# Openings of the two head attentions moved into the stages before them, and the program's first loads reordered

## The reference

```python
x = x + jnp.tanh(g_xattn[0]) * _L0_xattn_ref(_layernorm(x, axis=-1), ctx_4096, ...)   # windowed attention
x = x + jnp.tanh(g_ffn[0]) * _L0_ffn_ref(_layernorm(x, axis=-1), ...)                 # mixture, top 2 of 8
x = x + jnp.tanh(g_xattn[1]) * _L1_xattn_ref(_layernorm(x, axis=-1), ctx_4096, ...)   # 32 heads, 4 of keys
x = x + jnp.tanh(g_ffn[1]) * _L1_ffn_ref(_layernorm(x, axis=-1), ...)                 # mixture, threshold
x = x + jnp.tanh(g_xattn[2]) * _L2_xattn_ref(_layernorm(x, axis=-1), ctx_4096, ...)   # one text head
x = x + jnp.tanh(g_ffn[2]) * _L2_ffn_ref(_layernorm(x, axis=-1), ...)                 # ternary weights
x = x + jnp.tanh(g_xattn[3]) * _L3_xattn_ref(_layernorm(x, axis=-1), ctx_4096, ...)   # 32 heads, 8 of keys, normed
x = x + jnp.tanh(g_ffn[3]) * _L3_ffn_ref(_layernorm(x, axis=-1), ...)                 # soft mixture
```

## Time and profile before

| what | us |
|---|---|
| median of 3 runs (3540.18 to 3541.86) | 3541.75 |
| the profiled execution | 3532.72 |
| its span, first to last instruction | 3530.9 |
| TensorE busy in it | 3308.4 (94%) |
| VectorE busy | 1845.0 (52%) |
| ScalarE busy | 1480.9 (42%) |
| GpSimd busy | 1088.2 (31%) |

### The profile page before, as it was taken

The page is one execution under the profiler, slowest core; times in us unless marked ns, Lnnn a source line. Parts: engine busy times, 40 slices in busy tenths (PEclk is TensorE's granted clock), DMA queues, the critical chain, the costliest instruction groups (busy, mean ns, idle before and its releaser), DMA issues. The chain is left out here.

```text
span 3530.9 us, 50041 instructions
## 1 busy us (share of the span) xinstructions
PE 3308.4 (94%) x19010; PEld 2778.4 (79%) x19010; DVE 1845.0 (52%) x3681; ACT 1480.9 (42%) x3318; POOL 1088.2 (31%) x632
## 2 busy tenths in 40 slices
PE   6999988999999999999988875999999999999996
PEld 5888864888888888888864654888788878888885
DVE  5788764333433343333344465555655565555554
ACT  4444422444444444444432443444344444444443
POOL 4333312223322322322321212333333333333323
PEclk9999999999999999999999897999999999999998
DMA  2000001122222212112100202122212212222201
GB/s 100 1 1 1 1 22 64 64 64 66 72 66 67 72 60 66 66 61 66 54 28 28 95 12 87 63 66 66 83 62 66 84 60 67 70 66 66 72 30 54
DMA packets 56657, 199.64 MB, mean 57 GB/s; under 512 B 9088, under 2 KB 9856, under 8 KB 53120
## 3 DMA queue, kind: packets, MB, share of 16 engines
q1 hardware_dynamic: 56448, 196.80, 16.7%
HBM read 192.58 MB, written 4.19 MB: 56 GB/s over the span
## 5 line engine op out<-in xcount | busy, mean ns | idle before, releaser
L1562 POOL TENSOR_TENSOR h_wol<-h_ro,h_woh 128x1024 fp32r<-128x1024 f32 x128 | 314.3, 2456 | 609.2 <-ACT h_woh L1612 609.2
L2046 DVE COPY h_tf<-ps 128x512 f32<-128x512 f32 (+1 forms) x256 | 142.5, 557 | 613.3 <-PE ps L1827 613.3
L1558 POOL TENSOR_TENSOR h_wql<-h_rq,h_wqh 128x1024 fp32r<-128x1024 f32 x128 | 308.9, 2414 | 483.4 <-ACT h_wqh L1607 483.4
L2050 DVE TENSOR_TENSOR h_ol<-ps,h_oh 128x512 fp32r<-128x512 f32 x256 | 177.0, 691 | 527.1 <-ACT h_oh L1665 526.9
L131 PE MATMUL ps<-h_woh,h_oh 128*128 128x512 f32 x1024 | 427.5, 418 | 5.7 <-DVE h_ol L2050 5.7
L131 PE MATMUL ps<-h_Xh,h_wqh 128*128 128x512 f32 x1024 | 414.2, 404 | 1.8 <-ACT h_sq L1651 0.8
L133 PE MATMUL ps<-h_woh,h_ol 128*128 128x512 f32 x1024 | 404.9, 395 | 0.0
L132 PE MATMUL ps<-h_wol,h_oh 128*128 128x512 f32 x1024 | 403.6, 394 | 0.0
L133 PE MATMUL ps<-h_Xh,h_wql 128*128 128x512 f32 x1024 | 401.3, 392 | 0.0
L132 PE MATMUL ps<-h_Xl,h_wqh 128*128 128x512 f32 x1024 | 401.1, 392 | 0.0
L1716 ACT ACTIVATE h_ex<-ps,h_mx 128x128 f32<-128x128 f32 x512 | 181.4, 366 | 269.6 <-DVE h_mx L2086 269.6
(11 more groups left out here) (287 smaller groups left out, 6754.6 us busy)
## 6 DMA issues: line engine op xcount, KB each, us to landing
h_rq<-in_L_Wq SPq DMA_DIRECT2D x128, 512.0 KB, 3.5
h_ro<-in_L_Wo SPq DMA_DIRECT2D x128, 512.0 KB, 3.5
h_rk<-in_L_Wkv SPq DMA_DIRECT2D x48, 512.0 KB, 3.5
h_craw<-in_ctxT SPq DMA_DIRECT2D x8, 1024.0 KB, 5.3
cnat<-in_ctx SPq DMA_DIRECT2D x4, 1024.0 KB, 11.0
t_craw<-in_ctxT SPq DMA_DIRECT2D x4, 1024.0 KB, 5.2
t_cn<-in_ctx SPq DMA_DIRECT2D x4, 1024.0 KB, 5.8
out_rows<-x SPq DMA_DIRECT2D x16, 256.0 KB, 2.2
```

Source lines behind the costliest of these rows:

```text
L1558: nc.gpsimd.tensor_tensor(wql[:, par], rq[:, par], f(wqh[:, par]), ALU.subtract).then_inc(m["p_wq"], 1)
L1562: nc.gpsimd.tensor_tensor(wol[:, par], ro[:, par], f(woh[:, par]), ALU.subtract).then_inc(m["p_wo"], 1)
L2046: nc.vector.tensor_copy(tf[:], ps[:, TBK, 0:PT]).then_inc(m["v_t"], 1)
L2050: nc.vector.tensor_tensor(by_head(ol), ps[:, AB, :].rearrange("p (b h t) -> p b h t", h=2, t=S), f(by_head(oh)), ALU.subtract).then_inc(m[ ...
```

## The change

- The program's first loads: the first context group now comes before the weights, and TensorE waits for 11 small constants and six quarter weights; the output weights, the next group of x and the 13 other loads follow, with semaphores of their own (`l_wo`, `l_late`). ScalarE loads one table set for logarithm and exponential at the start, and Tanh of the gates moves into the loop, behind the second exponential of the first tile.
- `phase_heads` becomes a generator: up to `yield opening` it makes the tiles of the opening (`h_ch`, `h_cl`, `h_wkh`, `h_wkl`, `h_xn` and small ones) and an object whose methods issue the opening's loads, splits, statistics, root and scaled rows. The stage in front (mixture 0 for heads 1, the text stage for heads 3) calls them in its own queues; the rest comes behind the barrier. The semaphores of both head attentions live to the program's end.
- In the heads stage, the first half of the first keys no longer waits for `v_xl`, and with `norm` the second block of keys and values goes to another bank, so that it follows the first at once.
- In the text stage, keys and queries are now single f32 products without splits. Context has two buffers, and the feed-forward weights have buffers of their own, which later take the opening's loads.

```diff
+                        sp.dma_start(cnat[:, 0:NT], a["ctx"][0]).then_inc(l_ct[0], 16)
+                        weights(("q", "k", "v"), l_w)
                         for dst, src in loads:
                             sp.dma_start(dst, src).then_inc(l_c, 16)
+                        weights(("o",), l_wo)
+                        sp.dma_start(x[:, NT:2 * NT], a["x"][1]).then_inc(l_x[1], 16)
+                        for dst, src in late:
+                            sp.dma_start(dst, src).then_inc(l_late, 16)
...
+                        nc.scalar.preload_act_table_set(LN_EXP)
                         act_root(act, 0)
...
+                                    else:
+                                        act.wait_ge(l_late, 16 * len(late))
+                                        nc.scalar.activation(tg[:], gates[:], ACT.Tanh).then_inc(c_a, 1)
+                                        nc.scalar.preload_act_table_set(LN_EXP)
...
                                 nc.gpsimd.tensor_tensor(x[:, i], x[:, i], tbias[:], ALU.add).then_inc(p_xb, 1)
+                                if opening and i == NT - 1:
+                                    opening.pool_keys(pool)
+                                if opening and i in (2 * NT - 1, 3 * NT - 1):
+                                    opening.pool_context(pool, (0, 1) if i < 2 * NT else (2, 3))
...
+                                if g == 0:
+                                    opening.act_keys(act)
+                                if g in (1, 2):
+                                    opening.act_context(act, (2 * g - 2, 2 * g - 1))
+                                if g == G - 1:
+                                    opening.rows_root(act)
...
+                            elif opening:
+                                opening.rows_stats(dve)
                             weigh(g)
+                            if opening and not more:
+                                opening.rows_out(dve)
                         add_output(G - 1)
...
-                                    last = passes(pe, ps[:, 4 + e % 2, :], wh[:, 1, c, cols(e)], wl[:, 1, c, cols(e)], ch[:, c], cl[:, c],
-                                                  c == 0, c == NC - 1)
+                                    last = nc.tensor.matmul(ps[:, 4 + e % 2, :], wr[:, 1, c, cols(e)], craw[:, g % 2, c],
+                                                            start=(c == 0), stop=(c == NC - 1))
...
+                            elif g + 2 == G:
+                                opening.rows_stats(dve)
+                            else:
+                                opening.rows_out(dve)
                             dve.wait_ge(s_t, g + 1)
                             nc.vector.tensor_copy(tf[:], ps[:, 3, :].rearrange("p (j k) -> p j k", j=NT)).then_inc(v_t, 1)
-                            if g + 1 < G:
-                                low(g + 1)
...
+                    def loads(self, sp):
+                        sp.dma_start(self.rk.rearrange("p c n -> p (c n)"), wkv[0]).then_inc(m["l_kv"], 16)
+                        sp.dma_start(self.craw, a["ctxT"][0]).then_inc(m["l_ct"], 16)
...
+                                if half and at(it, 0):
+                                    pe.wait_ge(m["v_xl"], NT)
...
                             kv_rows(0)
+                            kv_rows(1, AB)
+                            pe.wait_ge(m["v_xl"], NT)
                             pe.wait_ge(m["p_wq"], 1)
                             head(0, 0, 0)
-                            pe.wait_ge(m["a_krv"], 1)
-                            kv_rows(1)
```

More of the change, by code:

```diff
@@ L68, in sem, with sem_to_the_end @@
             return s
+        def sem_to_the_end(name):
+            return top.enter_context(nc.semaphore(name))
         def end_phase():
@@ L438, in _ @@
                         act.wait_ge(l_c, 16 * len(loads))
-                        nc.scalar.activation(tg[:], gates[:], ACT.Tanh).then_inc(c_a, 1)
-                        nc.scalar.preload_act_table_set(LN_EXP)
                         act.wait_ge(p_z, 2)
@@ L568, in _ @@
                             sp.dma_start(bb[:], bias.unsqueeze(0).broadcast_to((P, D))).then_inc(l_b, 16)
-                        if store is not None:
-                            for i in range(NTILE):
-                                sp.wait_ge(v_x, i + 1)
-                                sp.dma_start(store[i // NT, :, i % NT], x[:, i]).then_inc(l_out, 16)
-                            sp.wait_ge(l_out, 16 * NTILE)
+                        if opening:
+                            opening.loads(sp)
                     if n_base:
@@ L1149, in _ @@
                                 out(g + 1, range(NC), s_k, a_k, kt, bk2)
-                                high(g + 1)
+                                rows_turned(g + 1)
                             if g:
                                 quants_out(g - 1)
+                            if g == 1:
+                                opening.act_keys(act)
+                            if g == 2:
+                                opening.act_context(act, range(NC))
+                                opening.rows_root(act)
                         gelus(G - 2)
@@ L1424, in phase_heads @@
+                opening = Opening(None if norm else craw[:], None if norm else rk[:])
+                yield opening
+                if norm:
+                    craw = tb("craw", [P, NC, TG])
+                    rk = tb("rk", [P, NC, 2 * HD])
+                rq, ro = tb("rq", [P, 2, NC, 2 * HD]), tb("ro", [P, 2, 2, D])
                 wqh, wql = (tb(n, [P, 2, NC, 2 * HD], F32R) for n in ("wqh", "wql"))
-                wkh, wkl = (tb(n, [P, NC, 2 * HD], F32R) for n in ("wkh", "wkl"))
                 Xh, Xl = (tb(n, [P, 2, NC, TG], F32R) for n in ("Xh", "Xl"))
-                ch, cl = (tb(n, [P, NC, TG], F32R) for n in ("ch", "cl"))
@@ L1529, in context @@
                             sp.dma_start(craw[:], a["ctxT"][g]).then_inc(m["l_ct"], 16)
-                        context(0)
-                        load(rk[:], wkv, 0, "l_kv")
                         load(rq[:, 0], wq, 0, "lq0")
```

265 lines of the change are left out of this document (138 added, 127 removed).

## The result

| | before | after |
|---|---|---|
| median of the runs | 3540.97 us | 3507.40 us |
| lowest to highest | 3535.16 to 3541.86 | 3503.82 to 3514.04 |
| profiled execution, span | 3530.9 us | 3512.1 us |

A forecast was written before the change was run, and what follows sets the result against it. TensorE, busy 94% of the span, bounds the kernel, so only its waits, low clock or work pay. Terms -5.4 - 13 - 4.5 + 11.9 + 2.7 - 17 = -25.3 us from 3541.75 give 3517; range 3505 to 3532.

The forecast's parts named there:

- rival 2: Text stage: the f32 products cost nothing, their added time falling into waits; D near 0, 3505 us; chance 0.12.
- B: Opening of the first head attention in the mixture before: key products sooner after the barrier; -13 us, bounds -9 and -14.
- D: Text stage, first to last scores: 96 dearer f32 products, less waits that come back; +11.9 us, bounds +8 and +16.7.
- F: Opening of the second head attention: turned keys at about 2177 instead of 2192.28; -17 us, bounds -12 and -19.
- A: Program's first loads: TensorE starts 7.6 us earlier, Tanh in the loop costs 2.2 us; -5.4 us.
- Rival 5: First tile: a table load holds ScalarE about as long again as its row shows; 2.8 us more, 3520; chance 0.05.
- the first half ends at 602.5, so it just fits: First head attention's first keys: low parts of the rows come at 602.3, before the first half ends at 602.5.
- C: Text stage's start: keys in f32 need no split, first scores come sooner; -4.5 us, bounds -3 and -6.
- E: Text stage's end: scaled rows stand on VectorE before the shares' copy; +2.7 us, bounds +1 and +3.5.
- 1: Across the changed places, waits move rather than go, a second engine being close behind; 14 us gained, 3531; chance 0.20.
- 3: Text stage's loop runs at 1.2 GHz: 82 us for all 96 products, 3599 us; chance 0.05.
- 4: An opening's splits or roots queue behind something late, delaying the barrier; some 20 us given back, 3537; chance 0.06.

The follow-up runs named there:

- A alone: The kernel before with only the first loads and Tanh as in the change: 3534.53 us against 3541.19, ratio 0.9991 (0.9974 to 1.0008).

## Why the prediction was right, and where by luck

The time lay 9.6 us under the forecast of 3517 and inside the range, but also just outside the forecast case's own 3510 to 3524, close to rival 2. The sign and the openings held; three terms were off by 6 to 8 us each (B promised too much, D and F too little) and cancelled in part. That the sum came within 10 us is luck to that extent.

**A, -5.4: the path was right, the worth is not settled.** TensorE started at 14.85 (15.0 forecast), the scores moved by 7.7 us (7.6), Tanh cost 1.1 to 2.4 (2.2). The medians gave -5 to -7, the ratio of A alone -3, with zero inside its interval. What was missing is the spread: this stage alone moves the kernel by 10 us between executions. Rival 5 is out: between the table load at 40.53 and the next activation at 41.83 stand 1.30 us, 0.02 us more than the load. The Trainium skill's drain (ScalarE: Activation LUTs, section "What ACT_TABLE_LOAD costs") shows nowhere in these rows.

**B, -13: 8 us too much** (-7.1 in the stage, +1.9 in the mixture). The first key product came 13.1 us sooner after the barrier (11.0 forecast; the transposes ran at the full clock, 1.94 us, where 3.67 was assumed). The step "the first half ends at 602.5, so it just fits" failed: the first half ended 4.75 us after the start instead of 7.5, and the low parts of the rows came at 8.15 instead of 7.3, so they were 3.4 us late. By the prediction's own sign ("wrong if the low parts of the rows are late in B") this term was wrong. It cost little: the second group of key products (619.17 before, 616.24 after) still came 12.2 us sooner after the barrier. The larger part of the miss comes from two effects that the working did not contain. "That hides" holds for the scaled rows (ready at 599.3, the addition at 599.87), but the splits in "stretches of tens of idle microseconds" held up GpSimd's queue, and the mixture took 1.9 us more. Of these, 0.9 was shown to come from GpSimd's additions beside VectorE, and 1.0 is open. And the tiles' new offsets cost 5.6 us in the stage.

**C, -4.5: -6.5.** The keys started where expected; their sixteen products took 15.8 us instead of 16.6, and the queries' sixteen ran in 14.0 us, near the lower end of 13.7 to 16.6.

**D, +11.9: +6.3,** under the lower bound of 8. The products' price was sound: 16 take 13.90 us, 0.869 each, 96 x (0.869 - 0.68) = +18, where the sum had 16.7 from 0.857 each. What failed is the share of the waits that comes back. Idle time fell by 8.1 us (13.5 to 5.5), where the estimate gave back 4.8: the waits for the key copies (2.9 us) went too, which the estimate did not list, and those for the turned rows fell by 4.1 us (3.5 forecast). TensorE's busy time grew by only 14.3 us, 3.7 less than the price; 1.2 of that is the clock, 0.99 before and 1.00 after, the rest is open:

```profile
1979.94:2101.55 121.61, 108.07 (x535) 80.93 (x535) 80.11 (x169) 57.68 (x96) 16.05 (x16) 0.99 0.07 27
```

```profile
1975.35:2103.22 127.87, 122.38 (x437) 62.11 (x439) 75.38 (x166) 57.03 (x95) 13.44 (x13) 1.00 0.12 46
```

**E, +2.7: +2.2,** and +2.6 in the wait itself.

**F, -17: -22.7,** beyond the bound of -19. Until the turned keys it was 17.7 us (15.1 forecast, since the normalised keys stood ready at 2176.7, 13.9 us after the start, and TensorE was at the full clock sooner). The low clock behind the old wait was worth 2.7 us more (1.9 forecast), and another 2.3 us came later in the stage: 1.3 between the first and the last copy of the shares, where TensorE's clock fell less often (0.98 from 2200 to 2300 us before, 1.00 after), and 1.0 behind the last copy, which is open. That term was not in the sum.

**Rivals.** 1: waits did move in B (3.4 us), nowhere else. 2: half true, as D shows. 3: the clock was 1.00 in the loop, and 0.90 over the whole text stage against 0.86 before. 4: the barrier behind the mixture came 0.4 us later after VectorE's last addition, no more.

## What to carry to other kernels

Opening a stage in the one ahead pays nearly the whole wait, but the next wait must be read with the gain already taken off, at the faster clock that the gain brings. A step that waits in a queue, even in an idle stretch, moves all that stands behind it. When tiles are added, look at the offsets of the operands of the products that run thousands of times, and compare stages, not totals, where one stage spreads by more than the change is worth.

## What the hardware showed that was not expected

- Two operands of a product 192 bytes apart modulo 2048: 233 ns from pass to pass; at the same offset mostly 227 or 228 ns (128x512, three passes). An unused tile of 1856 bytes gave 5.6 us back in one stage; 2.5 of them lie in such passes, the others in passes with equal offsets, which ran up to 3 ns slower in the mean. With the outputs' parts moved from 96 bytes to the same offset, the output products gained 3.5 ns each (5.4 us in 1536 passes).
- VectorE's operations on 128x4 elements take 0.17 us alone (0.23 at most, of 507) and took 0.63 and 0.70 beside GpSimd's additions, up to 1.20 elsewhere in the same trace.
- The same first stage in eight profiles, where TensorE has many short gaps: 486.7 to 499.8 us long, with a granted clock of 0.70 in one and 0.87 in another over the same 199 or so records.
